# Graph attention with the context made by rows: the softmax sums as one more column of the context product, projection and transposes of x one quad later

## Chip, core and metric

One core of a Trainium2 chip. The metric is device time in microseconds; a kernel's time is the median of several executions. Engines: TensorE (PE; its weight loads are shown apart as PEld), VectorE (DVE), ScalarE (ACT), GpSimd (POOL) and SyncE (SP), which issues most transfers. Each takes its own instructions in order and waits on semaphores.

## What is computed

x is 128 graphs of 128 nodes with 128 features, fp32; adj is a 0/1 matrix for each graph. Four layers follow each other, each as x = x + layer(layernorm(x)):

```
attention 1:  q,k,v = x W.T + b (4 heads of 32);  s = q k.T * 32**-0.5;  s = -1e9 where adj == 0
              c = softmax(s) v;  o = c Wo.T + bo;  layernorm(o) * gamma + beta
experts:      8 experts, best 2 of a router
attention 2:  q,k,v = x W (8 heads of 16); same masked softmax;  c Wo + bo
recurrent:    30 steps of tanh, silu, layernorm, a 128x128 product
```

The change touches the two attentions only.

## The kernel before

x stays in SBUF as x_sb. `graph_attention` is called twice, with heads=4 (PARTS = 1, normed) and heads=8 (PARTS = 2). It works on quads of 4 graphs, 32 quads; in the second attention a quad has two parts of 4 heads each. n numbers the sets of scores: n = k in the first attention, n = 2k and 2k + 1 in the second. Every engine runs a hand-written `body(k, par)` for each quad; `quads` unrolls the first and last quads and loops over the middle ones. The order inside a body is the order of that engine's queue, and the bodies overlap by semaphores alone.

PSUM has eight banks here: four hold the scores p_s (one for each of 4 heads, 4 graphs side by side), and p_w, p_z, p_x, p_y serve everything else in turn. What is in a bank must be read before the next product into it starts, and this sets much of the order.

The way of a quad: VectorE makes statistics of x (`stats_x`, L277 to L281) two quads ahead, GpSimd the power -1/2 of the variance (L214) and the mask from adj (L215). VectorE normalises x (`normalise_x`, four operations, L288), TensorE transposes it (L447), ScalarE copies it (L610), and q, k and v are made (L432, L436, L441; copies L581 or L584, L590 or L592 and L593, L599 or L603). `scores` lays the mask (L413) and q k.T (L419; 32-row tiles) into p_s. VectorE takes the row maxima (L295, one for each bank) and splits them into a high and a low bf16 part (L304, L309); TensorE transposes both parts in two halves into p_z and p_w (L453), VectorE copies them (L316), TensorE adds them negated to the scores (`shift_scores`, L460), and ScalarE takes the exponential (L575). TensorE transposes the probabilities bank by bank (L426) and ScalarE copies them into prob_t (L570).

From prob_t two products are made one set later. `sum_prob` (L466): a matrix of ones as stationary operand for each bank, so that p_y holds every sum 32 times over, in the layout of the context's transpose (rows are features, columns are nodes). `context_product` (L473): 32 columns of v as stationary operand, a column tile of the array for each bank, prob_t moving, into p_x, already transposed. VectorE inverts p_y (512 elements in each partition, L332) and multiplies (L338) into context_t; TensorE projects (L481) into p_y; VectorE adds the bias (L347, first attention) or adds to x (L344, second). The first attention goes on with statistics (L352, L356), power on GpSimd (L227), norm (L363) and GpSimd's three operations: times gamma, plus beta, plus x (L220, L222, L224). The second has one GpSimd addition (L231).

Body of VectorE before: statistics of x, maxima, inverse sums, norm of the projection of quad k-2, scaled context, norm of x for k+2, projection of k-1 taken and its statistics; in the second attention then the maxima of the other part and the norm of x. Body of TensorE: scores, last two transposes of the old probabilities between q and k, maxima, sums, shift, context, shift, v, x's transposes, projection of k-1, first two transposes of the new probabilities.

Of the kernel before, what the change touches and what calls it, by code (L numbers as in the profile page):

```python
# [17 lines left out]
ALU = mybir.AluOpType  # L18
ACT = mybir.ActivationFunctionType
AX = mybir.AxisListType  # L20
P = 128
# [4 lines left out]
def graph_attention(nc, env, tag, x_sb, adj, weights, heads, transposed, normed, masked_op, N_GRAPHS=128, x_in=None):  # L26
# [4 lines left out]

    D = P // heads
    PARTS = heads // 4
# [9 lines left out]
    with ExitStack() as ctx:  # L43
# [17 lines left out]
        ones = sb("ones", [P, PARTS, 32])  # L61
# [9 lines left out]
        v_sb = sb("v_sb", [P, 2, PARTS, QG, P])  # L71
# [5 lines left out]
        rden = sb("rden", [P, QUAD])  # L77
# [45 lines left out]
        s_den = sem("sums_ready")  # L123
        s_pv = sem("context_product")
        s_rden = sem("rden_ready")
        s_ctx = sem("context_t_ready")
# [20 lines left out]
        def quads(eng, body):  # L147

            for j in (-1, 0, 1):
                body(2 * j, 0)  # L150
                body(2 * j + 1, 1)
            with eng.Fori(2, QUADS // 2 - 1) as j:
                body(2 * j, 0)
                body(2 * j + 1, 1)
            for j in (QUADS // 2 - 1, QUADS // 2):
                body(2 * j, 0)
                body(2 * j + 1, 1)
# [8 lines left out]
        by_head = lambda v: v.rearrange("p (a h d) -> p a h d", h=2, d=D)  # L166
# [3 lines left out]
        with nc.Block() as block:  # L170
# [26 lines left out]
            def _(pool):  # L197
                nc.gpsimd.memset(split[:], 0.0).then_inc(s_fill, 1)
                if PARTS == 2:
                    nc.gpsimd.memset(ones[:], 0.0).then_inc(s_fill, 1)  # L200
                    nc.gpsimd.memset(v_sb[:], 0.0).then_inc(s_fill, 1)
                    pool.wait_ge(s_fill, 3)
                    for part in range(2):
                        nc.gpsimd.memset(ones[:, part, part * D:(part + 1) * D], 1.0).then_inc(s_fill, 1)
                else:
                    nc.gpsimd.memset(ones[:], 1.0).then_inc(s_fill, 1)
                pool.wait_ge(s_prep, n_prep)

                def body(k, par):
                    if live(k + 2):  # L210
# [6 lines left out]
                    if normed and live(k - 2):  # L217
                        x_quad = x_sb[:, bass.ds((k - 2) * QG, QG), :]
                        pool.wait_ge(s_fn, k - 1)
                        nc.gpsimd.tensor_tensor(proj_n[:], proj_n[:], quad_row(gamma), ALU.mult).then_inc(s_fp, 1)  # L220
                        pool.wait_ge(s_fp, 2 * (k - 2) + 1)
                        nc.gpsimd.tensor_tensor(proj_n[:], proj_n[:], quad_row(beta), ALU.add).then_inc(s_fp, 1)  # L222
                        pool.wait_ge(s_fp, 2 * (k - 2) + 2)
                        nc.gpsimd.tensor_tensor(x_quad, x_quad, proj_n[:], ALU.add).then_inc(s_done, 1)  # L224
                    if normed and live(k - 1):
                        pool.wait_ge(s_fvar, k)
                        nc.gpsimd.tensor_tensor(rstd_o[:], var_o[:], minus_half[:, 0:QG], ALU.pow).then_inc(s_frstd, 1)  # L227
                    if not normed and live(k - 1):
                        x_quad = x_sb[:, bass.ds((k - 1) * QG, QG), :]
                        pool.wait_ge(s_fin, k)  # L230
# [6 lines left out]
            def _(dve):  # L237
# [30 lines left out]
                dve.wait_ge(s_fill, 5 if PARTS == 2 else 2)  # L268
# [43 lines left out]
                def take_maxima(n, half):  # L312
# [3 lines left out]
                    nc.vector.tensor_copy(max_t[rows, :], (p_w if half else p_z)[rows, 0:P]).then_inc(s_mtc, 1)  # L316
# [17 lines left out]
                def normalise_context(k):  # L334
                    dve.wait_ge(s_pv, PARTS * (k + 1))
                    dve.wait_ge(s_rden, k + 1)
                    wait(dve, s_o, k)
                    nc.vector.tensor_tensor(context_t[:], p_x[:], rden[:], ALU.mult).then_inc(s_ctx, 1)  # L338

                def take_projection(k):  # L340
                    dve.wait_ge(s_o, k + 1)
                    if not normed:
                        x_quad = x_sb[:, bass.ds(k * QG, QG), :]
                        nc.vector.tensor_tensor(x_quad, x_quad, by_graph(p_y), ALU.add).then_inc(s_fin, 1)  # L344
                        return
                    wait(dve, s_fn, k)
                    nc.vector.tensor_tensor(proj[:], by_graph(p_y), quad_row(out_bias), ALU.add).then_inc(s_fin, 1)  # L347
# [19 lines left out]
                def body(k, par):  # L367
                    if live(k + 2):
                        stats_x(k + 2)
                    if live(k):  # L370
                        maxima(PARTS * k)
                    if live(k - 1):
                        invert_sums(k - 1)
                    if normed and live(k - 2):
                        normalise_projection(k - 2)
                    if live(k - 1):
                        normalise_context(k - 1)
                    if normed and live(k + 2):
                        normalise_x(k + 2)
                    if live(k - 1):  # L380
                        take_projection(k - 1)
                    if normed and live(k - 1):
                        stats_projection(k - 1)
                    if PARTS == 2 and live(k):
                        maxima(PARTS * k + 1)
                    if not normed and live(k + 2):
                        normalise_x(k + 2)

# [1156 lines left out]
```

## Time and profile before

| | |
|---|---|
| median of 3 runs | 3371.14 us (3370.3 to 3374.31) |
| profiled execution | 3371.62 us, its span 3369.7 us |
| busy PE, DVE, ACT, POOL | 2915.1, 2727.3, 2109.1, 1731.5 us |
| mean granted clock of TensorE | 0.917 |
| chain that ended last | DVE 30%, issue 9%, all in the recurrent layer's lines |

Busy time is an average over four stages with different limits, so the page's slices come first. Each digit is the busy share of a fortieth of the span, 84 us, in tenths; PEclk is the granted clock in tenths:

```profile
PE   5666666669999978888888856999999999999999
DVE  4777777668888866666666657999999999999999
PEclk8777777789999989999999977999999999999999
```

Slices 1 to 8 are the first attention, 9 to 14 the experts, 15 to 23 the second attention, the rest the recurrent layer. The page's chain of work covers the recurrent layer and says nothing of the attentions: there the timeline of one quad has to be read.

### The profile page before, as it was taken

The page shows a single profiled execution, that of the slowest core. Times are in us where ns is not written, and L with a number is a line of the kernel's source. Part 1 is how long each engine was busy: PE and PEld are TensorE (multiplying, and loading weights), DVE is VectorE, ACT ScalarE, POOL GpSimd, SP SyncE. Part 2 cuts the span into 40 slices and gives each one's busy share as a digit, 9 for nine tenths or more (in the row PEclk, how much of TensorE's full clock was granted, in tenths as well). Part 3 has the DMA queues.
Part 4 walks back from the last instruction along what each step waited for, and adds up shares of the span by engine and source line. Part 5 has one row for each costly group of instructions (what it writes and reads, how often), then busy time and mean ns, then how long its engine had stood idle before and what let it go on. Part 6 is the DMA issues. An engine that isn't in the chain of part 4 may idle for free. (4 is left out here: it accounts for less than half of the span.)

```text
span 3369.7 us, 70085 instructions
## 1 busy us (share of the span) xinstructions
PE 2915.1 (87%) x20479; PEld 1907.5 (57%) x20479; DVE 2727.3 (81%) x7398; ACT 2109.1 (63%) x3936; POOL 1731.5 (51%) x1148
## 2 busy tenths in 40 slices
PE   5666666669999978888888856999999999999999
PEld 3444444458888855555555535555555555555556
DVE  4777777668888866666666657999999999999999
ACT  2333333324444444445454537999999999999995
POOL 2333333333333321212111125999999998888883
PEclk8777777789999989999999977999999999999999
DMA  4000000000000000000000002555555555555555
GB/s 127 13 12 12 12 13 15 0 14 0 0 0 0 0 24 11 13 9 12 9 12 9 6 3 76 195 195 195 197 198 201 201 201 198 196 197 195 197 197 176
DMA packets 132579, 281.68 MB, mean 84 GB/s; under 512 B 11760, under 2 KB 69152, under 8 KB 132512
## 3 DMA queue, kind: packets, MB, share of 16 engines
q1 hardware_dynamic: 115616, 272.44, 23.5%
q10 hardware_dynamic: 16896, 8.39, 0.9%
q8 instruction: 37, 0.61, 0.1%
q14 instruction: 30, 0.25, 0.0%
HBM read 270.49 MB, written 10.29 MB: 83 GB/s over the span
## 5 line engine op out<-in xcount | busy, mean ns | idle before, releaser
L1168 POOL TENSOR_TENSOR d_g<-d_g,d_rb 128x1024 f32<-128x1024 f32 x464 | 1083.9, 2372 | 127.9 <-DMA d_rb<-d_rstd_rows 112.7
L1369 PE MATMUL d_p_y<-d_g,d_w_main 128*128 128x512 f32 x1856 | 952.6, 595 | 0.0
L1383 PEld LDWEIGHTS d_p_gt<-ident,d_g 128*128 128x128 f32 x3840 | 450.4, 142 | 541.8 <-ACT d_g L1428 380.4
L1247 DVE BATCH_NORM_STATS2 d_stats<-d_p_gt 128x6 f32<-128x256 f32 x1920 | 713.0, 407 | 23.3 <-PE d_p_gt L1383 23.2
L1428 ACT ACTIVATE d_g<-d_th,d_bias 128x512 f32<-128x512 f32 x928 | 667.0, 719 | 12.1 <-DVE d_th L1240 0.9
L1240 DVE SCALAR_TENSOR_TENSOR d_th<-d_th,d_p_y 128x512 f32<-128x512 f32 x960 | 634.7, 661 | 4.1 <-ACT d_th L1424 4.1
L1424 ACT ACTIVATE d_th<-d_p_y,d_bias 128x512 f32<-128x512 f32 x928 | 625.6, 674 | 0.3 <-PE d_p_y L1369 0.3
L1383 PE MATMUL d_p_gt<-ident,d_g 128*128 128x128 f32 x3840 | 592.6, 278 | 0.1
L295 DVE TENSOR_REDUCE a_row_max<-a_p_s 128x4 f32<-128x512 f32 x384 | 253.6, 682 | 231.6 <-PE a_p_s L419 231.6
L570 ACT COPY a_prob_t<-a_p_w 128x512 f32<-128x512 f32 x288 | 169.5, 588 | 406.0 <-PE a_p_w L426 405.9
L214 POOL TENSOR_TENSOR a_rstd<-a_var,minus_half 128x4 f32<-128x4 f32 x64 | 65.3, 1020 | 670.9 <-PE a_p_s L419 630.0
L897 DVE SCALAR_TENSOR_TENSOR x_sb<-m_p_y,m_combine,x_sb 128x128 f32 (+1 forms) x1024 | 310.9, 342 | 68.8 <-PE m_p_y L939 56.0
L986 ACT ACTIVATE m_hidden<-m_p_h,m_cols 128x512 f32<-128x512 f32 x256 | 176.5, 689 | 225.9 <-PE m_p_h L931 225.9
L575 ACT ACTIVATE a_prob<-a_p_s 128x512 f32<-128x512 f32 x384 | 208.3, 594 | 134.9 <-PE a_p_s L460 134.9
L1369 PEld LDWEIGHTS d_p_y<-d_g,d_w_main 128*128 128x128 f32 x1856 | 280.1, 191 | 6.3 <-issue 4.7
L939 PEld LDWEIGHTS m_p_y<-m_w_sb,m_hidden 128*128 128x128 f32 x2048 | 266.4, 191 | 25.6 <-issue 3.6
L939 PE MATMUL m_p_y<-m_w_sb,m_hidden 128*128 128x128 f32 x2048 | 271.0, 275 | 0.0
L447 PE MATMUL a_p_w<-ident,a_xn 128*128 128x128 f32 x256 | 57.0, 362 | 210.2 <-DVE a_xn L288 210.2
L332 DVE RECIPROCAL a_rden<-a_p_y 128x512 f32<-128x512 f32 x64 | 214.9, 3358 | 12.0 <-PE a_p_y L466 10.0
L426 PE MATMUL a_p_w<-ident,a_prob 128*128 128x128 f32 x1152 | 209.1, 311 | 4.8 <-ACT a_prob_t L570 3.3
L481 PE MATMUL a_p_y<-a_w_o,a_context_t 128*128 128x128 f32 x512 | 104.8, 371 | 101.3 <-DVE a_context_t L338 101.3
L426 PEld LDWEIGHTS a_p_w<-ident,a_prob 128*128 128x128 f32 x1152 | 145.3, 157 | 64.7 <-ACT a_prob_t L570 44.0
(192 smaller groups left out, 4216.6 us busy)
## 6 DMA issues: line engine op xcount, KB each, us to landing
d_rb<-d_rstd_rows SPq DMA_DIRECT2D x464, 512.0 KB, 5.5
a_adj_in<-in_adj_dram SPq DMA_DIRECT2D x64, 256.0 KB, 2.8
out_dram<-d_out_sb ACTq DMA_DIRECT2D x32, 256.0 KB, 2.4
d_rstd_rows<-d_rstd_row SPq DMA_DIRECT2D x116, 16.0 KB, 1.4
m_w_sb<-in_L_ffn_w_dram SPq DMA_DIRECT2D x2, 512.0 KB
x_sb<-in_x_dram SPq DMA_DIRECT2D x1, 256.0 KB, 2.8
a_w_raw<-in_L_gnn_Wq_dram SPq DMA_DIRECT2D x2, 64.0 KB, 2.1
a_w_raw<-in_L_gnn_Wk_dram SPq DMA_DIRECT2D x2, 64.0 KB, 2.1
```

Source lines behind the costliest of these rows:

```text
L295: ins = nc.vector.tensor_reduce(out=row_max[:, t], in_=p_s[:, t], axis=AX.X, op=ALU.max)
L332: nc.vector.reciprocal(rden[:], p_y[:]).then_inc(s_rden, 1)
L426: last = nc.tensor.transpose(bank[:, graph(g)], prob[:, t, g, :], ident[:])
L897: last = nc.vector.scalar_tensor_tensor(out=x_tile, in0=p_y[:, e % 2, t, :], scalar=combine[:, par, t, e:e + 1], in1=x_tile, op0=ALU.mult, ...
L939: last = nc.tensor.matmul(p_y[:, e % 2, t, :], hidden[:, e % 2, t * P:(t + 1) * P], w2_sb[:, e, :], start=True, stop=True)
L1168: nc.gpsimd.tensor_tensor(g[:, c, :], g[:, c, :], rb[:, buf, :], ALU.mult).then_inc(s_gs, 1)
L1240: nc.vector.scalar_tensor_tensor(out=th[:, b, cols(u)], in0=th[:, b, cols(u)], scalar=0.01, in1=p_y[:, b, cols(u)], op0=ALU.mult, op1=ALU. ...
L1247: ins = nc.vector.bn_stats(stats[:, q % 2, (j * CT + t) // 2].rearrange("p a s -> p (a s)"), p_gt[:, t * P:(t + 2) * P].rearrange("p (a c) ...
L1369: nc.tensor.matmul(p_y[:, c % 2, cols(u)], w_main[:], g[:, c, cols(u)], start=True, stop=True).then_inc(s_y, 1)
L1383: ins = nc.tensor.transpose(p_gt[:, t * P:(t + 1) * P], g[:, c, t * P:(t + 1) * P], ident[:])
L1424: nc.scalar.activation(th[:, b, cols(u)], p_y[:, b, cols(u)], ACT.Tanh, bias=col).then_inc(s_th, 1)
L1428: nc.scalar.activation(g[:, c, cols(u)], th[:, c % 2, cols(u)], ACT.Silu, bias=col).then_inc(s_g, 1)
```

## The change

- The context is made by rows: 128 columns of probabilities (transposed, one graph, one head) are the stationary operand, and the moving one is v of that head with a column of ones behind it (v_ones, 33 or 17 columns). The result has nodes as rows, and the last column of each head is the sum. `sum_prob` and the matrices of ones go. The products go in two halves to p_w and p_z (first attention) or into p_w by part (second).
- VectorE inverts the sums (8 or 16 elements a partition) and scales, in two shares, into `context`; four transposes and a ScalarE copy make context_t (`transpose_context`, `take_context`).
- The projection is made at quad k-2 and taken at k-3 (first) or k-2 (second); the norm of the projection, its statistics and GpSimd's operations follow at k-3 and k-4, GpSimd's three now ahead of the power and mask in its body. Statistics of x are made three quads ahead in the first attention and the norm of x stands behind the maxima.
- The transposed maxima of both halves, x's transposes and q (in the second attention v) use p_y, k and v (second: k), the transposed context and the projection p_x. The bodies are written out apart for the two attentions.

Cut to its core:

```diff
-        v_sb = sb("v_sb", [P, 2, PARTS, QG, P])
+        v_ones = sb("v_ones", [P, 2, QG, heads, VW])
-        rden = sb("rden", [P, QUAD])
+        rden = sb("rden", [P, 2, 8 * PARTS])
+        context = sb("context", [P, 2, QG, P])
...
-                def invert_sums(k):
-                    dve.wait_ge(s_den, PARTS * (k + 1))
-                    nc.vector.reciprocal(rden[:], p_y[:]).then_inc(s_rden, 1)
...
+                    dve.wait_ge(s_pv, 2 * k + share + 1)
+                    nc.vector.reciprocal(inverse, src[:, :, :, D]).then_inc(s_rden, 1)
+                    dve.wait_ge(s_rden, 2 * k + share + 1)
+                    wait(dve, s_ct, k - 1)
+                    each = rden[:, share].rearrange("p (g h a) -> p g h a", h=4, a=1)
+                    nc.vector.tensor_tensor(dst, src[:, :, :, 0:D], each.broadcast_to([P, 2 * PARTS, 4, D]),
+                                            ALU.mult).then_inc(s_norm, 1)
...
-                        last = nc.tensor.matmul(p_y[tile(t), :], ones[:, part, :], prob_t[:, t],
-                                                start=part == 0, stop=part == PARTS - 1)
...
+                        for t in range(4):
+                            last = nc.tensor.matmul(dst[:, i, t], prob_t[:, t, g, :], v_ones[:, par, g, PARTS * t + part],
+                                                    start=True, stop=True)
...
+                def transpose_context(k, par):
+                    pe.wait_ge(s_norm, 2 * (k + 1))
+                    for g in range(QG):
+                        last = nc.tensor.transpose(p_x[:, graph(g)], context[:, par, g, :], ident[:])
+                    last.then_inc(s_ct, 1)
```

VectorE's bodies after:

```
first:   take_projection(k-3), maxima(k), normalise_x(k+2), normalise_context(k-1, 0), (k-1, 1),
         stats_projection(k-3), stats_x(k+3), normalise_projection(k-3)
second:  maxima(2k), normalise_x(k+1), normalise_context(k-1, 1), stats_x(k+2), take_projection(k-2),
         maxima(2k+1), normalise_context(k, 0)
```

TensorE's bodies after:

```
first:   scores, context transposed (k-2), probabilities 2 (k-1), q (k+1), probabilities 3, k (k+1), maxima 0,
         context graphs 0 and 1 (k-1), shift 0, maxima 1, context graphs 2 and 3, shift 1, v (k+1), x (k+2),
         probabilities 0 and 1 (k), project (k-2)
second:  scores, context transposed (k-2), probabilities 2, v (k), probabilities 3, maxima 0, context, shift 0,
         maxima 1, context, shift 1, project (k-2), x (k+1), probabilities 0 and 1;
         scores, probabilities 2, q (k+1), probabilities 3, k (k+1), maxima 0, context, shift 0, maxima 1, context,
         shift 1, wait for the scaled context, probabilities 0 and 1
```

## Rows read from the trace of the kernel before

**Rows 1.** One tile (inverse sums), both attentions: ns min/median/max, first and last start us.
```profile
L332 DVE RECIPROCAL a_rden<-a_p_y x32: 3356/3358/3358, 57.9 to 677.3; 128x512 f32<-128x512 f32 x32
...
L332 DVE RECIPROCAL a_rden<-a_p_y x32: 3356/3358/3358, 1246.7 to 1978.9; 128x512 f32<-128x512 f32 x32
```
**Rows 2.** Timeline, first attention, one quad: start, length us, engine, idle before.
```profile
300.50 3.36 DVE L332 RECIPROCAL a_rden<-a_p_y 128x512 f32<-128x512 f32 x1
...
303.77 1.02 DVE L363 TENSOR_SCALAR a_proj_n<-a_proj,a_stats_o,a_rstd_o 128x128 f32<-128x128 f32 x4
...
304.88 1.26 POOL L220 TENSOR_TENSOR a_proj_n<-a_proj_n,a_gamma 128x512 f32<-128x512 f32 x1 [5.92 <-DVE a_proj_n L363]
305.31 3.71 DVE L288 TENSOR_SCALAR a_xn<-x_sb,a_stats,a_rstd 128x128 f32 x4
...
307.68 1.26 POOL L224 TENSOR_TENSOR x_sb<-x_sb,a_proj_n 128x512 f32 x1 [0.20 <-POOL a_proj_n L222]
...
309.07 1.11 PE L447 MATMUL a_p_w<-ident,a_xn 128*128 128x128 f32 x4 [6.52 <-DVE a_xn L288]
...
316.21 1.29 DVE L295 TENSOR_REDUCE a_row_max<-a_p_s 128x4 f32<-128x512 f32 x2 [1.11 <-PE a_p_s L419]
...
318.86 0.24 PE L453 MATMUL a_p_z<-ident_bf,a_split 128*64 128x128 bf16 x1
...
320.96 3.36 DVE L332 RECIPROCAL a_rden<-a_p_y 128x512 f32<-128x512 f32 x1
```
**Rows 3.** Stretches: us, busy PE, PEld, DVE, ACT, POOL (count), PEclk, DMA, GB/s.
```profile
300.50:321.00 20.50, 13.98 (x133) 9.46 (x128) 14.83 (x28) 6.99 (x14) 7.76 (x6) 0.75 0.04 13
302.90:309.10 6.20, 0.03 (x1) 0.03 (x1) 6.12 (x10) 0.28 (x1) 3.78 (x3) 0.62 0.00 0
309.10:314.60 5.50, 5.50 (x23) 4.69 (x24) 2.09 (x6) 1.76 (x3) 0.90 (x1) 0.50 0.00 0
...
1579.00:1602.90 23.90, 20.16 (x232) 12.54 (x225) 15.08 (x32) 11.70 (x24) 4.23 (x3) 0.93 0.04 11
...
1608.30:1611.70 3.40, 3.40 (x13) 1.95 (x11) 0.69 (x1) 1.17 (x2) 0.00 (x0) 0.50 0.00 0
```
**Rows 4.** Timeline of TensorE, second attention, one quad.
```profile
1589.37 1.02 PE L432 MATMUL a_p_y<-a_xn_t,a_w_q 128*128 128x512 f32 x2
...
1590.23 0.63 PE L426 MATMUL a_p_w<-ident,a_prob 128*128 128x128 f32 x4
...
1596.05 1.03 PE L413 MATMUL a_p_s<-a_mask,ident_bf 128*128 128x512 bf16 x4
...
1597.00 1.17 PE L419 MATMUL a_p_s<-a_k_t,a_q_t 32*128 32x128 f32 x32
...
1601.96 0.39 PE L460 MATMUL a_p_s<-a_selector,a_max_t 32*128 32x512 bf16 x2
...
1602.45 1.08 PE L473 MATMUL a_p_x<-a_prob_t,a_v_sb 128*32 128x128 f32 x32
...
1607.27 1.13 PE L481 MATMUL a_p_y<-a_w_o,a_context_t 128*128 128x128 f32 x8 [2.83 <-DVE a_context_t L338]
```
**Rows 5.** Timeline of TensorE, mixture of experts: the router's product.
```profile
762.00 0.96 PE L963 MATMUL m_p_lg<-m_cols,m_xn_t 128*128 128x8 f32 x8
...
762.84 0.48 PE L929 MATMUL m_p_h<-m_xt_hi,m_w_lo 128*128 128x512 f32 x1
```
**Rows 6.** Timeline of VectorE, second attention.
```profile
1592.19 0.17 DVE L304 TENSOR_SCALAR a_split<-a_row_max 128x8 bf16<-128x8 f32 x1
...
1592.48 1.08 DVE L309 SCALAR_TENSOR_TENSOR a_split<-a_row_max,a_split 128x8 bf16<-128x8 f32 x1
...
1594.22 1.12 DVE L288 TENSOR_SCALAR a_xn<-x_sb,a_stats,a_rstd 128x128 f32 x4
...
1595.49 0.76 DVE L277 BATCH_NORM_STATS2 a_stats<-x_sb 128x6 f32 x2 [0.15 <-DVE a_xn L288]
```
**Rows 7.** Timeline of ScalarE, second attention: the copy of v.
```profile
1599.77 0.65 ACT L603 COPY a_v_sb<-a_p_z 128x256 f32<-128x256 f32 x2 [0.38 <-PE a_p_z L441]
```

More of the change, by code:

```diff
@@ L151, in quads @@
                 body(2 * j + 1, 1)
-            with eng.Fori(2, QUADS // 2 - 1) as j:
+            with eng.Fori(2, QUADS // 2 - 2) as j:
                 body(2 * j, 0)
                 body(2 * j + 1, 1)
-            for j in (QUADS // 2 - 1, QUADS // 2):
+            for j in range(QUADS // 2 - 2, QUADS // 2 + 2):
                 body(2 * j, 0)
@@ L198, in _ @@
                 nc.gpsimd.memset(split[:], 0.0).then_inc(s_fill, 1)
[L199 to L206, printed above, removed]
+                nc.gpsimd.memset(v_ones[:], 1.0).then_inc(s_fill, 1)
                 pool.wait_ge(s_prep, n_prep)
                 def body(k, par):
+                    if normed and live(k - 4):
+                        x_quad = x_sb[:, bass.ds((k - 4) * QG, QG), :]
+                        pool.wait_ge(s_fn, k - 3)
+                        nc.gpsimd.tensor_tensor(proj_n[:], proj_n[:], quad_row(gamma), ALU.mult).then_inc(s_fp, 1)
+                        pool.wait_ge(s_fp, 2 * (k - 4) + 1)
+                        nc.gpsimd.tensor_tensor(proj_n[:], proj_n[:], quad_row(beta), ALU.add).then_inc(s_fp, 1)
+                        pool.wait_ge(s_fp, 2 * (k - 4) + 2)
+                        nc.gpsimd.tensor_tensor(x_quad, x_quad, proj_n[:], ALU.add).then_inc(s_done, 1)
                     if live(k + 2):
@@ L593, in take_k, with take_v @@
                         nc.scalar.activation(k_t[:, 1], p_x[:], ACT.Copy, scale=part_of[:, 1:2]).then_inc(s_k, 1)
[L595 removed]
+                def take_v(k, par, bank):
                     act.wait_ge(s_vmm, k + 1)
[L597 to L604 removed]
+                    wait(act, s_pv, 2 * (k - 1))
+                    nc.scalar.copy(v_ones[:, par, :, :, 0:D],
+                                   bank[:].rearrange("p (g h c) -> p g h c", g=QG, h=heads)).then_inc(s_v, 1)
                 def take_xn(k):
@@ new lines, in take_xn, with take_context, first_body @@
+                    nc.scalar.copy(xn_t[:], p_y[:]).then_inc(s_xtc, 1)
+                def take_context(k):
+                    act.wait_ge(s_ct, k + 1)
+                    wait(act, s_o, k)
+                    nc.scalar.copy(context_t[:], p_x[:]).then_inc(s_ctc, 1)
+                def first_body(k, par):
+                    if live(k - 1):
+                        take_prob(k - 1, 0)
+                        take_prob(k - 1, 1)
+                    if live(k - 2):
+                        take_context(k - 2)
+                    if live(k - 1):
+                        take_prob(k - 1, 2)
+                    if live(k + 1):
+                        take_q(k + 1)
+                    if live(k - 1):
+                        take_prob(k - 1, 3)
+                    if live(k + 1):
+                        take_k(k + 1)
+                    if live(k):
+                        for t in range(4):
+                            exponentials(k, t)
+                    if live(k + 1):
+                        take_v(k + 1, 1 - par, p_x)
+                    if live(k + 2):
+                        take_xn(k + 2)
```

410 lines of the change are left out of this document (235 added, 175 removed).

## The prediction

> **What bounds the kernel now.** I read the page's 40 slices first: the two attention stages (about 31 to 692 us and 1213 to 1995 us) are where TensorE is least busy. The change touches only them, so the 500 us of the mixture of experts and the 1330 us of the recurrent stage stay as they are. The view of one tile, the inverse sums, gives one reciprocal per quad of graphs, so its first and last start measure a quad: 31 steps from 57.9 to 677.3 us are 19.98 us each in the first attention, 31 steps from 1246.7 to 1978.9 us are 23.62 us each in the second [rows 1].
>
> Then I followed one quad in the timeline. In the first attention it is a loop that hands over between VectorE and TensorE, with nothing beside it [rows 2]. From the reciprocal at 300.50 VectorE never rests until 309.0: reciprocal 3.36, norm of the old projection (1.02), context scaled, and x normalised, which takes 3.71 us. Only then can TensorE transpose x (309.07, after 6.52 us idle), and behind it in its queue stand projection, two transposes of the probabilities, masks and scores. Those end at 316.2, where VectorE starts the row maxima; these end in the next reciprocal at 320.96. The sum is the period, 20.46 us.
>
> Three things in this loop are dearer than they need be. The reciprocal runs over 512 elements a row. The four normalisations of x take 3.71 us since three GpSimd operations of 1.26 us run in the same time (304.88 to 308.94 [rows 2]); in the second attention, where none does, the same four take 1.12 us [rows 6]. And TensorE, after its rest, works from 309.1 to 314.6 at a granted clock of 0.50, so 1.2 instead of 2.4 GHz [rows 3].
> By the Trainium skill (GPSIMD Engine Reference, Specifications) GpSimd shares its SBUF interfaces with VectorE and contends with VectorE instructions in a 2-port mode or with two SBUF inputs; the trace agrees (3.71 against 1.12 us), also for an 8-element operation with two such inputs, which took 1.08 us beside a GpSimd operation [rows 6].
>
> The second attention has two sets of scores per quad and is nearer to TensorE's own work: 20.16 us busy of 23.90 [rows 3]. Its one large hole is 2.83 us before the projection, which waits for reciprocal and scaled context [rows 4], and 3.4 us at half clock after it [rows 3].
>
> **The change, part by part.** (1) Removed: the context product in 32-column tiles (32 matmuls, 1.08 us with their tail [rows 4]), the sums by a matrix of ones (8 matmuls, which I take as long), and the reciprocal over 512 elements. Per quad TensorE loses 2.0 us in the first attention and 4.0 in the second, VectorE 3.36 in each.
>
> (2) Added: the context product with 128 columns of probabilities as weights and 33 (or 17) moving columns. In fp32 every product is two instructions, so 32 weight loads and matmuls per set of scores. No such row exists in attention; the nearest on both sides are the router's product with 8 moving columns, 8 pairs from 762.00 to 762.84 [rows 5], so 0.105 us a pair at full clock, and the transposes with 128 columns, 4 from 1590.23 within 0.63 us with their tail [rows 4], 0.11 a pair. The ends agree: the weight load sets the pace. 16 pairs are 1.7 us, and 0.25 before the next, differently tiled product can start: 1.95 us for each half, 3.9 per set, against 2.0 for what it replaces.
> The Trainium skill (TensorEngine Tiling, When to Use Tiling) advises the reverse of this step: with 32 moving columns swap the operands and use column tiling four times. By its factor of four the product would go from 1.0 to 4.0 us, which the pace of rows 5 bears out; it speaks against this half of the change in the stage that TensorE bounds.
>
> (3) Added: 4 transposes of the context (0.48), a ScalarE copy (about 0.6, as v's in [rows 7]), and on VectorE per share a reciprocal of 8 or 16 elements and a scaling of 256. The trace has no reciprocal of this size; the bounds are 0.17, an 8-element operation [rows 6], and 3.36. With 3.36/512 = 6.6 ns an element added to 0.17 I take 0.2 and 0.25, nearer to the row of that size. The scaling of 256 elements is 0.42, half of a 512-element pass (two in 1.29 [rows 2]) and its start. VectorE in the first attention: 14.83 us a quad [rows 3], less 3.36, less 2.6 (x beside no GpSimd work), plus 0.9, gives 9.8.
>
> (4) Moved: x's normalisation, its transposes and the projection. First attention, TensorE's queue at full clock [rows 4]: masks 0.95 (1596.05 to 1597.00), scores 1.1, six groups of 4 transposes 2.9, q and k 0.86 each, shift and transposed maxima twice 0.49 (1601.96 to 1602.45), context 3.9, v and projection 0.9 and 0.96 (8 pairs each): 13.4 us. I walked the waits along it: from the end of the scores to the first transposed maxima TensorE now has 3.2 us of work, VectorE needs 2.65 + 0.15 for the split maxima (316.21 to 318.86 [rows 2]), so this wait closes; v, projection and the last transposes (2.8 us) cover the scaled contexts; the probabilities' copies on ScalarE (about 8 us a quad) keep pace.
> What is late next is GpSimd. Its gamma, beta and x operations now wait for the projection's norm at the end of VectorE's body and run for 4.05 us into the next maxima. There the split of the maxima (a few elements, with SBUF inputs) is held as in rows 6. The loop: from the first to the second transposed maxima 2.4 (context half, shift), their copy and x 1.8, two scaled contexts 1.4, statistics of the projection 1.0 (0.76 [rows 6] and the variance), GpSimd's power 1.1, norm 1.1, GpSimd's three 4.1, then the held split, a row maximum and the low part 1.0: 13.9, which I round to 13.95 for hand-overs. I take **13.95 us**, bounds 13.4 (no contention) and 14.95 (the power of GpSimd that follows holds it for 1.0 more).
>
> Second attention, same durations. First half: 2.05 for masks and scores; from there to the context product 3.4, since v's copy (0.65 [rows 7]) and the last probabilities' copy behind it on ScalarE are late by 0.7; context, shifts, maxima 4.7; projection, transposes of x and of two tiles 2.4: 12.6. Second half: 2.05, then 2.95, then 4.4 up to the last context product's issue; its result must be inverted and scaled before the bank is free (0.25 + 0.42 + hand-overs), 0.55 us in which TensorE stands, then 1.0: 11.2. Total **23.8 us**, equal to the 23.85 of a steady quad before: the 2.83 us hole and the half clock go, and 3.9 us of added weight loads, 0.5 of transposes and the new waits take their place.
>
> (5) The end: the last quads now drain one body later, and GpSimd does three quads' work of 4 us with a power between. From the last probabilities to the end of the first attention I count 25 us against about 18 (the last reciprocal starts at 677.3). Plus 7 us, once. In the second the added and removed pieces cancel. Filling v_ones hides behind the weights' transfers.
>
> **The sum**, against the profiled execution's 3371.6 us (3371.14 is the median): first attention 31 x 19.98 = 619.4 before; 31 x 13.95 = 432.5 after, less 4 for the last quads, which lack projections of a next one: 191 saved, less 7 is 184. Second: 0. 3371.6 - 184 = **3188 us** (13.4 us and no stalls in the second: 3188 - 17 - 30 = 3141).
>
> **Rivals.** *A, the forecast*, chance 0.55.
> *B, the clock falls at the new product.* In the trace the clock fell while TensorE rested and stayed at half through 5.5 us of full work before it rose (302.9 to 309.1, then to 314.6 [rows 3]). No stretch there is filled with matmuls of 33 columns behind 128-column loads, where the array streams for a quarter of the time; the chip may take that for rest. In the second attention one low stretch lasts 3.4 us [rows 3], costing half of it, 1.7. Three such groups per pair of quads make 93; if two thirds of them trigger one: 93 x 0.67 x 1.7 = 105 us, 3293. Chance 0.26.
> By the Trainium skill (TensorE: Matmul & The Clock Gate, Part 1) a monitor sets the clock by how busy the array has been; whether a weight load counts, no row here shows.
> *C, the in-order queues lose more than I found*: one further microsecond in each quad of both stages, for instance the held split in the first and the scaled context in the second: 62 us, 3250. Chance 0.11.
> *D, slower*: the clock is low throughout each group, so a group costs 3.9 more: first attention 17.9, second 31: 3371.6 - 65 + 7 + 229 = 3543. It decides from 184/93 = 2.0 us a group, so if more than about half of each runs at 1.2 GHz. Against it: the low level in rows 3 follows rest, not work. Chance 0.06.
> *E, the change doesn't do what it says*: a reciprocal costs 3.36 us whatever its size; no other size stands in the trace. Then VectorE alone needs 9.8 + 6.3 = 16.1 us in the first attention, 16.4 with waits, and the second takes 3.1 more: 31 x (3.6 - 3.1) is gained, 7 lost, about 3363. Against it: VectorE's other operations shrink with their size (0.17 for 8 elements [rows 6], 0.65 for 512 [rows 2]). Chance 0.02.
>
> **How the numbers follow.** The likeliest is A, 3188, whose own range is 3141 to 3235. To hold 8 in 10 the range must reach B's centre: 3141 to 3300; beyond lie D, E and the upper part of B. A difference within 0.2% (7 us) can't be told from none. Faster: A, B, C and part of E, 0.92; same 0.02; slower 0.06.
>
> **What would show it.** A quad of 14 us in the first attention, the granted clock at 1.00 throughout, the four normalisations of x in 1.1 us, VectorE waiting before the maxima rather than TensorE before x. The 32 pairs of a context product in 3.5 to 3.9 us; twice that, or a granted clock of 0.50 behind them, speaks for B or D. In the second attention a period near 23.8 with a wait of about half a microsecond before the transposes that follow the last context product. The forecast fails first if the clock does not hold or if the queue's waits in the second attention are longer than my 1.3 us.

## The result and the profile after

The kernel with the change takes 3431.7 us (median; 3429.55 to 3438.22) beside 3372.72 us of the kernel before: a ratio of 1.018 (95% interval 1.016 to 1.020). It is 59 us slower where 184 us less were forecast.

The stages tell that two things happened at once:

| stage | before | after | change |
|---|---|---|---|
| first attention | 689.9 us | 566.0 us | -123.9 |
| experts | 510.6 | 510.8 | +0.2 |
| second attention | 784.4 | 970.5 | +186.1 |
| recurrent | 1382.3 | 1380.1 | -2.2 |

A steady quad, by the starts of the row maxima of quads 5 to 25, went from 20.48 to 15.88 us in the first attention and from 23.77 to 29.23 us in the second. The page's slices of after show where (same columns as those of before ahead of the prediction):

```profile
PE   6999996999998999999999985999999999999999
DVE  4666664888886434444444437999999999999999
PEclk8888886999998778777777766999999999999999
```

Slices 1 to 7 are the first attention, 8 to 12 the experts, 13 to 24 the second. TensorE is now busy throughout both attentions, VectorE 60% of the first and 40% of the second: the loop of [rows 2] is gone. But PEclk, 9 in most slices of the second attention before, is 7 in most of them. The view of stretches says the same with numbers (us; busy of PE, PEld, DVE, ACT, POOL with counts; granted clock; DMA share; GB/s), here the middle of each attention, of after:

```profile
50.00:530.00 480.00, 479.14 (x3571) 389.78 (x3569) 288.01 (x851) 222.11 (x391) 220.88 (x170) 0.82 0.05 15
1110.00:2040.00 930.00, 898.35 (x6526) 714.80 (x6524) 376.64 (x993) 386.40 (x691) 126.42 (x90) 0.76 0.03 8
```

and the same of before:

```profile
50.00:650.00 600.00, 413.79 (x3638) 278.25 (x3637) 431.78 (x787) 206.20 (x357) 221.46 (x171) 0.75 0.04 12
1240.00:1960.00 720.00, 606.49 (x6700) 383.95 (x6697) 452.25 (x903) 353.08 (x671) 123.85 (x88) 0.93 0.03 10
```

After the change TensorE rests for 0.9 us of 480 and 32 us of 930, and its mean granted clock is 0.82 and 0.76. The granted clock has only two levels here, 1.00 and 0.50; in these stretches it is at the half level for 36% and 47% of the time (before: 49% and 13%). In the first attention the low clock of before lay behind a rest, as in [rows 3]; now it lies between instructions that follow each other without a gap.

Where it falls shows in the timeline of a quad. First attention, after (start, length, engine, operation; in brackets idle time before it and what ended it):

```profile
309.28 1.97 PE L484 MATMUL a_p_w<-a_v_ones,a_prob_t 128*128 128x33 f32 x16
...
311.68 1.97 PE L484 MATMUL a_p_z<-a_v_ones,a_prob_t 128*128 128x33 f32 x16
...
312.11 1.11 DVE L284 TENSOR_SCALAR a_xn<-x_sb,a_stats,a_rstd 128x128 f32 x4
313.26 0.21 DVE L336 RECIPROCAL a_rden<-a_p_w 128x8 f32<-128x8 f32 x1
313.50 0.42 DVE L340 TENSOR_TENSOR a_context<-a_p_w,a_rden 128x256 f32<-128x256 f32 x1
...
313.90 2.06 PE L455 MATMUL a_p_x<-a_w_v,a_xn_t 128*128 128x128 f32 x8
...
315.75 1.06 PE L461 MATMUL a_p_y<-ident,a_xn 128*128 128x128 f32 x4
```

and the granted clock of the stretches from the scores on, in the same columns as above, with the low stretch of the quad before ahead of them:

```profile
298.20:303.80 5.60, 5.60 (x28) 5.60 (x28) 2.78 (x10) 3.19 (x6) 3.44 (x3) 0.51 0.00 0
...
304.82:309.28 4.46, 4.46 (x51) 2.99 (x50) 3.15 (x7) 2.30 (x5) 3.55 (x3) 1.00 0.00 0
309.28:313.90 4.62, 4.62 (x39) 4.02 (x38) 2.48 (x11) 1.71 (x3) 0.00 (x0) 1.00 0.19 57
313.90:317.20 3.30, 3.30 (x17) 3.30 (x16) 3.01 (x12) 2.02 (x4) 1.04 (x1) 0.51 0.00 0
317.24:320.40 3.16, 3.16 (x42) 2.49 (x45) 1.10 (x3) 1.26 (x3) 2.54 (x2) 0.98 0.00 0
```

In this quad the two context halves themselves run at full clock, each in 1.97 us with its tail (1.95 were forecast). Behind them TensorE runs at 0.51, the 1.2 GHz level, with no idle time in between: v takes 2.06 us (a projection of 8 pairs, each a weight load and its matmul, took 1.13 in [rows 4]) and four transposes 1.06 (0.63 there). In the second attention the clock can fall within the product. TensorE of after:

```profile
1564.71 1.96 PE L484 MATMUL a_p_w<-a_v_ones,a_prob_t 128*128 128x17 f32 x16 [0.17 <-ACT a_prob_t L651]
...
1567.38 3.60 PE L484 MATMUL a_p_w<-a_v_ones,a_prob_t 128*128 128x17 f32 x16
...
1571.44 2.08 PE L498 MATMUL a_p_x<-a_w_o,a_context_t 128*128 128x128 f32 x8
```

The same 16 pairs take 1.96 us at full clock and 3.60 us at half.

How long the clock stays low varies from quad to quad. Between 50 and 530 us there are 30 low stretches, one in each quad: 20 of 6.8 us and 10 of 3.4. Quads with a short one, like the one shown, take 14.8 us from row maxima to row maxima, the others 16.4. On VectorE everything is as cheap as forecast: x's four normalisations 1.11 us beside 3.71 in [rows 2], the small reciprocals 0.21 us at their longest in this quad beside 3.36 in [rows 1].

### The profile page after: what moved, and what is told of

Read it like the earlier page. It is cut to its first block and busy times, and to the rows that moved or that the text cites. A ratio compares the mean times of both kernels' runs of the same rounds, so it can differ in the third digit from the quotient of the medians.

```text
span 3429.9 us, 69233 instructions
## 1 busy us (share of the span) xinstructions
PE 3255.9 (95%) x19967; PEld 2345.0 (68%) x19967; DVE 2485.2 (72%) x7526; ACT 2144.2 (63%) x3968; POOL 1732.3 (51%) x1145
## 5 line engine op out<-in xcount | busy, mean ns | idle before, releaser
L484 PE MATMUL a_p_w<-a_v_ones,a_prob_t 128*128 128x17 f32 (+1 forms) x2560 | 374.9, 293 | 7.0 <-ACT a_prob_t L651 7.0
L484 PEld LDWEIGHTS a_p_w<-a_v_ones,a_prob_t 128*128 128x128 f32 x2560 | 358.4, 224 | 21.2 <-ACT a_prob_t L651 11.9
L651 ACT COPY a_prob_t<-a_p_w 128x512 f32<-128x512 f32 x192 | 112.9, 588 | 108.4 <-PE a_p_w L442 107.5
L312 DVE CAST a_max_t<-a_p_y 64x128 bf16<-64x128 f32 x192 | 56.2, 293 | 158.4 <-PE a_p_y L467 158.4
L442 PE MATMUL a_p_w<-ident,a_prob 128*128 128x128 f32 x768 | 156.2, 340 | 13.6 <-DVE a_context L340 13.6
L691 ACT COPY a_context_t<-a_p_x 128x512 f32<-128x512 f32 x64 | 37.5, 586 | 203.3 <-PE a_p_x L492 203.3
```

The lines of the kernel that those rows point to most:

```text
L484: last = nc.tensor.matmul(dst[:, i, t], prob_t[:, t, g, :], v_ones[:, par, g, PARTS * t + part], start=True, stop=True)
```

## Experiments

**1. More moving columns, and nothing else.** If the array's short streaming behind long weight loads lowers the clock, wider moving operands should raise it again, at no cost as long as the weight load sets the pace. v_ones gets a tail, and each product moves 128 (or 64) columns from its head on; what it writes too far right is overwritten by the next product.

```diff
-        v_ones = sb("v_ones", [P, 2, QG, heads, VW])
+        v_ones = sb("v_ones", [P, 2, QG * heads * VW + COLS - VW])
...
-                            last = nc.tensor.matmul(dst[:, i, t], prob_t[:, t, g, :], v_ones[:, par, g, PARTS * t + part],
+                            last = nc.tensor.matmul(bank[:, at:at + COLS], prob_t[:, t, g, :], v_ones[:, par, of:of + COLS],
```

COLS = 128:

> The changed kernel, but each product of the context takes 128 moving columns instead of 33 or 17: the v and ones of the head and whatever stands behind them. The columns beyond the head's own are overwritten by the next product into the bank, or never read, so what is computed stays the same, and so do the counts of instructions, weight loads and waits. In the changed kernel's trace the clock was at half in 36% of the first attention and 48% of the second, and it fell in the second half of nearly every context product, although TensorE was issuing without a rest. Theory 1 (the clock falls because the array has few moving columns behind each weight load): a 128-column pair has the same pace as a short one, 0.11 us, so the products take the same 1.9 us at full clock, and the clock stays at 1.00: 15.7 us a quad becomes about 14.0 in the first attention and 29.3 becomes 23.8 in the second, together 3432 - 54 - 170 = 3208 us (3190 to 3235). Theory 2 (the clock falls for another reason: waits at the ends of the products, or the many weight loads themselves): within 10 us of 3432. Theory 3 (the order and the waits of the queues cost the time, and the clock is a by-product): at most 30 us better than 3432.

Measured: 3172.37 us (3170.93 to 3173.37), 0.941 of the kernel before (0.939 to 0.942). That is Theory 1, and 18 us better than the low end of its range. First attention 493.3 us, second 782.4; quads 13.55 and 23.65 us, where 14.0 and 23.8 were expected. In the middle stretches below the clock is at half for 2 us of 410 and for none of 680; what is left of the low clock lies at the stages' ends. The stretches in the middle of each attention, padded kernel:

```profile
50.00:460.00 410.00, 406.36 (x3574) 315.99 (x3573) 305.26 (x851) 214.96 (x391) 220.36 (x170) 1.00 0.06 18
1060.00:1740.00 680.00, 648.91 (x5974) 508.19 (x5974) 349.41 (x922) 346.72 (x634) 119.49 (x85) 1.00 0.04 11
```

and its rows for the product and what follows it:

```profile
300.73 2.05 PE L486 MATMUL a_p_z<-a_v_ones,a_prob_t 128*128 128x128 f32 x16
...
302.71 0.39 PE L476 MATMUL a_p_s<-a_selector,a_max_t 32*128 32x512 bf16 x2
...
303.03 1.16 PE L457 MATMUL a_p_x<-a_w_v,a_xn_t 128*128 128x128 f32 x8
```

Four or seven times as many columns move, and the shift behind the product starts 1.98 us after its first pair instead of 1.90 (309.28 to 311.18 in the kernel after). Dearer by 0.13 us a set (1.95 and 1.98 us for the two halves, 1.90 each before), the padded kernel is 259 us faster than the change as it was made. The counts and the order of the instructions are the same and only the width differs, so what the narrow products cost comes through the clock. TensorE now rests for 3.6 us of 410 in the first attention: that stage is bound by TensorE's own queue. From v to the masks, the stretch that ran at half clock, the padded kernel takes 3.20 us (303.03 to 306.23); the kernel after took 4.85 in the quad shown (313.90 to 318.75) and 6.01 in the one before it (297.85 to 303.86). The padded kernel beats both the kernel before and the change as made, and none of the runs that follow gave a faster one that computes everything.

COLS = 64:

> The same with 64 moving columns. Theory 1: somewhere from e1 (if 64 is enough to hold the clock) to halfway back: 3208 to 3320 us, and the share of time at half clock tells which. Theory 2 and 3: as the changed kernel, 3432 within 10.

Measured: 3219.62 us (3215.11 to 3221.48), 0.955 (0.953 to 0.957), inside Theory 1's range; first attention 491.5 us, second 826.6. In their middle stretches (50 to 460 and 1060 to 1780 us) the clock is at half for 0.2% and 12% of the time:

```profile
1060.00:1780.00 720.00, 688.93 (x6030) 545.34 (x6029) 351.82 (x925) 350.09 (x638) 120.91 (x86) 0.94 0.04 10
```

With 64 columns the clock holds in the first attention and not always in the second, where two sets of products stand in a quad. In the stand-alone stretch of experiment 3, it held throughout with 64 columns; what decides in the second attention isn't settled.

**2. The stages apart.** The first attention as changed, the second as before; once with the narrow product, once padded to 128.

```diff
-    graph_attention(nc, env, "a1_", ...)
+    graph_attention_2(nc, env, "a1_", ...)
```

> The change in the first attention alone; the second is the one of the kernel before. From the two traces the first attention went from 689.9 to 566.0 us (124 less) and the second from 784.4 to 970.5 (186 more). If the stages are independent, as their barriers suggest: 3372 - 124 = 3248 us (3242 to 3254). A rival in which the first attention's gain hangs on something shared (code loading, the state of the clock at a stage's start) would give over 3260.

Measured: 3250.94 us (3249.49 to 3252.36), 0.964 (0.962 to 0.966): stages of 567.0 and 786.8 us, inside the expected 3242 to 3254.

> The first attention changed and with 128 moving columns as in e1, the second as before. Theory 1: e3 less 54 us, 3194 (3180 to 3210), with a quad of 14.0 us in the first attention, which is also what the forecast's loop over GpSimd's three operations gives. Theory 2 and 3: as e3, 3248. If the quad comes out at 13.4 instead of 14.0, GpSimd's hold on VectorE is not in the loop.

Measured: 3178.43 us (3177.18 to 3178.77), 0.942 (0.941 to 0.944): stages of 492.1 and 788.7 us, just below Theory 1's 3180 to 3210. The quad of 13.55 us fell between the two values that were to decide about GpSimd's hold; experiment 4 decides it. The stages are independent within 5 us. Narrow, the second attention of the change costs 181 us (3431.7 - 3250.9); padded, it is worth 6 us (3178.4 - 3172.4). So what the prediction gave the second attention, 23.8 us a quad and neither gain nor loss, holds once the clock does (23.65).

**3. The clock by itself.** The kernel before with a stretch of TensorE alone between second attention and recurrent layer: fp32 products of a 128-column stationary and a moving operand of c columns, back to back with no wait in them, 120 products (240 pairs) of a width with 80 products of 128 columns ahead of each.

```diff
+            for count, widths in segments:
+                for n in range(count):
+                    c = widths[n % len(widths)]
+                    last = nc.tensor.matmul(p_c[:, 0:c], x_sb[:, n % 8, :], x_sb[:, 8 + n % 8, 0:c], start=True, stop=True)
```

> The kernel before, with a stretch of TensorE work of its own between the second attention and the recurrent layer; it only times itself, its results are not used. Stretches of 120 fp32 products (240 weight loads of 128 columns and matmuls) with 17, 33, 48, 64 and 96 moving columns, each behind 80 products of 128 columns; at the end 160 products that alternate 4 of 17 with 4 of 128, and 160 that alternate 16 with 16. No semaphore, no other engine and no rest is in it. Theory 1 (moving columns behind a weight load decide the clock): every pair takes 0.11 us at full clock whatever its width; the granted clock falls to 0.50 within the stretches of 17 and 33 and stays at 1.00 at 96 and 128; 64, which held in the first attention of e2 and partly fell in the second, lies at the edge; alternating 4 with 4 holds, 16 with 16 falls. Theory 2 (waits or rests in the attention's queue): 1.00 in all of them, since nothing waits. The stretch takes about 340 us if the clock holds, more where it falls.

Measured: one run, 3793.99 us, 420 more than the kernel before beside it, where the stretch was expected to take about 340 if the clock held. The stretches, in the columns as above: 17, 33, 48, 64 and 96 columns, then 4 products of 17 and 4 of 128 in turn, then 16 and 16 in turn:

```profile
2003.80:2051.10 47.30, 47.30 (x243) 47.30 (x241) 0.00 (x0) 0.00 (x0) 0.00 (x0) 0.54 0.00 1
2071.25:2117.80 46.55, 46.55 (x243) 46.55 (x241) 0.00 (x0) 0.00 (x0) 0.00 (x0) 0.55 0.00 1
2137.10:2184.50 47.40, 47.40 (x243) 47.40 (x241) 0.00 (x0) 0.00 (x0) 0.00 (x0) 0.54 0.00 1
2204.50:2231.25 26.75, 26.75 (x243) 26.75 (x241) 0.00 (x0) 0.00 (x0) 0.00 (x0) 1.00 0.00 1
2249.20:2275.90 26.70, 26.70 (x242) 26.70 (x241) 0.00 (x0) 0.00 (x0) 0.00 (x0) 1.00 0.00 1
2293.80:2329.60 35.80, 35.80 (x323) 35.80 (x323) 0.00 (x0) 0.00 (x0) 0.00 (x0) 1.00 0.00 1
2347.40:2391.30 43.90, 43.90 (x322) 43.90 (x322) 0.00 (x0) 0.00 (x0) 0.00 (x0) 0.81 0.00 1
```

TensorE and its weight loads are busy for all of each stretch, so nothing rests. 240 pairs with 64 or 96 columns take 26.7 us, 0.111 us a pair, at 1.00; with 17, 33 or 48 columns they take 46.6 to 47.4 us, at 0.54 or 0.55. So Theory 2 is refuted, and Theory 1 came as expected at 17, 33, 96 and in both mixtures. The number of moving columns is all that tells the first five stretches apart. As a pair takes the same 0.111 us with 64 as with 96, these runs don't separate the number of columns from the share of the time in which they stream. It isn't each product for itself: with four narrow ones between four wide ones the clock held, with 16 between 16 it was at half for 17.1 of 43.9 us. In the kernel after, the narrow ones come 8 products (16 pairs) at a time with shift and maxima between, and there it fell too.

**4. GpSimd's hold on the split of the maxima.** GpSimd's work can hold an operation of VectorE's, which then doesn't end before GpSimd's does ([rows 6]). In the forecast the first attention ends in a loop through GpSimd (13.95 us a quad), not in TensorE's own 13.4. Padded kernel with GpSimd's addition of beta left out of the first attention (the output lacks beta):

```diff
-                        nc.gpsimd.tensor_tensor(proj_n[:], proj_n[:], quad_row(beta), ALU.add).then_inc(s_fp, 1)
```

> e1 with GpSimd's addition of beta left out in the first attention (so beta is missing from the result): two operations of 1.27 us instead of three run into VectorE's maxima. If GpSimd's hold on VectorE (the 1.03 us split of 8 elements in e1's quad, and TensorE's 0.2 us wait behind it) is in the loop, as forecast, the quad of the first attention goes from 13.55 to 13.4: 32 x 0.15 = 5 us, and 1.3 once at the end, so e1 less 6 (3164 to 3168). If not: within 2 us of e1.

Measured: 3166.11 us (3165.24 to 3166.84), 0.939 (0.937 to 0.940), a quad of 13.39 us. That is 0.16 us a quad less than padded, about 5 of the 6 us, as expected. The hold is in the loop, but TensorE's queue, 13.4 us by the forecast, is nearly as long as that loop. In the padded kernel it is seen here:

```profile
309.59 1.27 POOL L215 TENSOR_TENSOR x_sb<-x_sb,a_proj_n 128x512 f32 x1 [0.20 <-POOL a_proj_n L213]
...
309.87 1.03 DVE L302 TENSOR_SCALAR a_split<-a_row_max 128x8 bf16<-128x8 f32 x1 [0.15 <-DVE a_row_max L293]
...
311.61 0.11 PEld L469 LDWEIGHTS a_p_y<-ident_bf,a_split 128*64 128x64 bf16 x1 [0.90 <-DVE a_split L307]
```

An 8-element operation takes 1.03 us beside a GpSimd operation and ends with it, at 310.9 (0.17 without, [rows 6]), and the maxima's weights wait 0.90 us; most of that stands in front of work that TensorE still had in its matmul queue (L452, 310.52 for 1.02 us).

The padded kernel with GpSimd's three operations behind power and mask instead of ahead of them:

```diff
-                    if normed and live(k - 4):
-                        x_quad = x_sb[:, bass.ds((k - 4) * QG, QG), :]
...
+                    if normed and live(k - 4):
+                        x_quad = x_sb[:, bass.ds((k - 4) * QG, QG), :]
```

> e1 with GpSimd's three operations on the projection put back behind the power and the mask in its body, as in the kernel before. They then run from about 3.1 us behind the scores' end to 7.1 and meet the norm of x at 5.9, which they hold for a microsecond or more, but the split of the maxima is free. My loop says that the norm of x has that microsecond to spare before TensorE's transposes of x, so the quad becomes 13.4: 3 to 6 us less than e1. The rival, that a held norm of x is what made the kernel before slow and does so again: the quad grows by a microsecond, 30 us more than e1.

Measured: 3175.54 us (3174.16 to 3176.92), 0.941 (0.940 to 0.942), a quad of 13.60 us. Neither the expected gain nor the rival's loss came. The hold moved with them. VectorE of this kernel:

```profile
301.82 2.12 DVE L286 TENSOR_SCALAR a_xn<-x_sb,a_stats,a_rstd 128x128 f32 x4
...
312.32 1.28 DVE L302 TENSOR_SCALAR a_split<-a_row_max 128x8 bf16<-128x8 f32 x1
```

x's normalisation now takes 2.12 us in place of 1.11, and a split is still held (1.28): in both places that were tried, the 4 us of GpSimd work lie beside something of VectorE's.

**5. What the dear reciprocal alone was worth.** The kernel before, with its order and its tiled context product; the reciprocal covers 16 of the 512 elements, and the other inverses are one, so the context is not normalised there.

```diff
-                    nc.vector.reciprocal(rden[:], p_y[:]).then_inc(s_rden, 1)
+                    nc.vector.reciprocal(rden[:, 0:16], p_y[:, 0:16]).then_inc(s_rden, 1)
```

> The kernel before, with the inverse of the sums taken over 16 of its 512 elements (the other inverses stay at one, so the context is not normalised): nothing else changes, TensorE's queue least of all. It measures how much of the change's gain is the dear reciprocal on the loop, apart from the new order. If the reading of the two timelines of before is right, 3.1 us leave the loop of the first attention (20.5 to 17.4 a quad, or down to 15.5 where TensorE's shorter rest keeps its clock up) and TensorE's 2.8 us hole before the projection in the second closes, with the half clock behind it (23.8 to 19.4): 3372 less 99 less 140 = 3133 us, from 3065 to 3185. If something else in the queue is late at once (the rival by which the change's gain came from its new order): 3300 or more.

Measured: 3116.03 us (3113.68 to 3116.62), 0.924 (0.922 to 0.925), inside the expected 3065 to 3185: stages of 563.0 and 653.7 us, quads of 16.66 and 19.65. The reciprocal took 3.10 us less (3.36 to 0.26), the quads 3.8 and 4.1 us less. The middle of the second attention of this kernel:

```profile
1120.00:1710.00 590.00, 559.22 (x6607) 350.29 (x6608) 354.24 (x891) 346.52 (x662) 123.93 (x88) 1.00 0.04 12
```

The hole in front of the projection [rows 4] and the half clock behind it [rows 3] went together: 1.00, where it was 0.93. That fits the quads' losing more than the reciprocal did; in the first attention, too, the mean clock rose, from 0.75 to 0.86. Set beside this kernel, the padded change shows what its two halves are worth: in the first attention it is 3.1 us a quad better than this kernel (13.55 against 16.66); in the second it is 4.0 us worse (23.65 against 19.65). The prediction counted 3.9 us of added weight loads and 0.5 of transposes there, which fits; but the two kernels also differ in their order, so the split isn't shown. In the second attention, then, the change spends on TensorE all that the cheap reciprocal gains.

**6. The inverse on ScalarE.** So I tried to have that cheap inverse with the tiled product: first attention padded, second as before, with 1/sum made on ScalarE as a logarithm and an exponential of its negative, between the second and third exponential of a set.

```diff
-                    nc.vector.reciprocal(rden[:], p_y[:]).then_inc(s_rden, 1)
+                    nc.scalar.activation(lnden[:], p_y[:], ACT.Ln).then_inc(s_lnd, 1)
...
+                    nc.scalar.activation(rden[:], lnden[:], ACT.Exp, scale=-1.0).then_inc(s_rden, 1)
```

> A version out of what the runs showed: the first attention as in e1, the second as in the kernel before, with its inverse of the sums made on ScalarE (logarithm from PSUM, exponential of its negative: two operations of about 0.6 us between the second and the third exponential) instead of VectorE's reciprocal of 3.36 us. e8 gave 19.65 us a quad in the second attention with a short reciprocal. ScalarE is busy 12 of 23.8 us there, so the two operations find room; the scaled context comes about 1 us later than in e8: 19.7 to 20.7 us a quad. 3172 - 782 + 660 = 3050 us (3040 to 3090). If logarithm and exponential need a table load at each change (1.28 us by the load seen once in the experts' stage, two for each quad): up to 3125. If the place in ScalarE's queue holds up the next exponentials: 3100.

Measured: 3227.22 us (3222.59 to 3228.61), 0.957 (0.955 to 0.959); the second attention is 840.4 us long, 52 us more than with the reciprocal (experiment 2), and its middle is at half clock for 20% of the time (14% there). A miss: 3050 us were expected, and 3125 with table loads. Part of the reason stands in ScalarE's timeline:

```profile
1279.44 1.28 ACT L614 ACT_TABLE_LOAD   x1
1280.73 0.60 ACT L614 ACTIVATE a_lnden<-a_p_y 128x512 f32<-128x512 f32 x1
1281.35 1.28 ACT L617 ACT_TABLE_LOAD   x1
1282.64 0.63 ACT L617 ACTIVATE a_rden<-a_lnden 128x512 f32<-128x512 f32 x1
```

The two functions cost the 1.2 us that were counted, and each brings a table load of 1.28 us, 52 of them in 26 quads. For 3.8 us a quad ScalarE takes nothing else, and the last two banks of probabilities wait in its queue. The quad is 5.9 us longer than in experiment 5 (25.59 against 19.65); the loads take 2.6 us of ScalarE's time a quad, and how the 5.9 divide between them, the waits in the queue and the lower clock wasn't tested. The Trainium skill (ScalarE: Activation LUTs, Table sets: the hidden batching unit) says that exponential and logarithm share one set and need one load; this trace shows one at each change between them. Other places for the pair weren't tried.

## Why the prediction was wrong

It failed in one step: the sum of part (4) takes every duration at full clock, and no term stands for what the new product does to the clock. The runs show that term as 259 us, more than the 200 that the rest of the change saves (3372.7 - 3172.4). In order of its parts:

**What bounds the kernel** was read rightly. With the loop gone and the clock held, the first attention fell from 20.48 to 13.55 us a quad. The 500 and 1330 us given to the other two stages are 510.6 and 1382.3 in the table above; neither enters the sum.

**Part (2), the price of a pair**, was right at full clock and left out what the pairs do to the clock. 1.95 us a half were forecast; 1.97 are measured with its tail, and 1.90 up to the next product. The router's product [rows 5], from which the price came, is 8 pairs with 8 columns; no row had a long run of narrow products, and the text said so under B. All durations of part (4) were taken at full clock, and of all assumptions in the sum this one weighed most.

**Part (3)** held: reciprocals 0.2 and 0.25 forecast, 0.21 and 0.26 measured, scaling 0.42 and 0.42. The view of the inverse's tile, of after (ns min/median/max, first and last start):

```profile
L336 DVE RECIPROCAL a_rden<-a_p_w x96: 207/257/258, 59.0 to 2040.7; 128x16 f32<-128x16 f32 x64, 128x8 f32<-128x8 f32 x32
L340 DVE TENSOR_TENSOR a_context<-a_p_w,a_rden x96: 423/425/426, 59.3 to 2041.0; 128x256 f32<-128x256 f32 x96
```

**Part (4)** held once the clock did: 13.95 forecast and 13.55 measured, 23.8 and 23.65. (The terms written down for the second attention's second half add up to 10.95 us, not 11.2, so its quad would be 23.5; that is as near.) Within the first, the loop through GpSimd was given 0.55 us above TensorE's own 13.4; experiment 4 shows 0.16. The wait before the transposes behind the last context product was forecast at about half a microsecond and is 0.56 and 0.57 us in the padded kernel's timeline (0.35 and 0.56 in that of after).

**Part (5)**, plus 7 and less 4 us at the ends: the first attention of the padded kernel is 196.6 us shorter than before. 184 were forecast. By first and last start, as in [rows 1], a quad fell from 19.98 to 13.39 us (31 steps from 60.1 to 475.2), 204 us in all, so the ends lost 8, where 3 (7 less 4) were counted. The 13.95 was set against a mean over all steps (19.98), so its counterpart is 13.39: the quad was 0.56 us too long, 17 us in all, of which the ends took back 5.

**The sum** of forecast A comes near the padded kernel: 3188 us against 3172. For the change as made it misses 244 us: 259 for the clock, less 15.

**Rival B** is what happened, with the right mechanism and two wrong sizes. It had a low stretch of 3.4 us behind two of three groups, each costing half of it, 1.7 us: 105 us in all, and a chance of 0.26. Measured are 259 us over 93 groups, 2.8 each: by stages (566.0 - 493.3) / 31 = 2.3 us in the first attention, (970.5 - 782.4) / 62 = 3.0 in the second. The first wrong size is how many groups bring the clock down: not two of three but practically each (30 low stretches in the 30 quads of the first stretch shown above, one a group in the second too). The other is how long it stays down. The 3.4 us came from a stretch at half clock that follows a rest [rows 3]; here it is 5.7 us a group on average in the first attention (36% of 15.88) and 6.9 in the second (47% of 29.23, over two groups), and half of that, 2.8 and 3.4 us, is what it can cost at most.

**Rival D**, slower, named the point at which the sign turns, 2.0 us a group, and rightly: the measured 2.8 lies above it, between B's 1.7 and D's own 3.9. What I held against it, that the low level in [rows 3] follows rest and not work, was true of the rows and no argument: none of them had this kind of work. D at 0.06 and a range that ended at B's centre were therefore too low: the range left out what B costs once its size is off by a factor of two.

The Trainium skill (TensorE: Matmul & The Clock Gate, Why this matters for your kernels) advises, for matmuls with few rows (small M), another loop or padding M, since the clock otherwise falls and rises with each tile. What is padded here is another size, the moving columns, and TensorE hardly waits (0.9 us of 480), so the runs neither test that advice nor its reason.

**Rival C** (longer queues' waits) did not come: the padded quads are shorter than forecast (13.55 and 23.65 us). **Rival E**, a reciprocal that costs 3.36 us whatever its size, is refuted by the 0.21 us.

**The advice on tiling** that the prediction weighed (the Trainium skill, TensorEngine Tiling, When to Use Tiling: swap the operands and tile) agrees with experiment 5: in the second attention the tiled product takes 19.65 us a quad once the reciprocal is cut short, and the product by rows 23.65. That kernel doesn't normalise its context, and experiment 6 found no way to do so at that price.

## What to carry over

A price per instruction that is read at full clock is only half of a price: of a new kind of TensorE work ask also what it leaves the array doing, and where long weight loads come with few moving columns, look at the granted clock behind them before anything else. Where the weight load sets the pace, padding the moving operand with columns that are overwritten costs next to nothing, and here it turned a ratio of 1.018 into 0.941. Where the bounds of a mechanism lie on both sides of the sign, a range must reach to its far end, not to the centre of its mild case.

## What the runs showed of the hardware

- TensorE without any rest was at 1.2 GHz for 43.2 of 47.3, 41.6 of 46.6 and 43.4 of 47.4 us in the stretches whose products move 17, 33 and 48 columns, and at 2.4 GHz throughout in those with 64 and 96 (experiment 3). In [rows 3] the half clock had followed a rest.
- At full clock a pair of an fp32 weight load of 128 columns and its matmul takes 0.111 us whether it moves 64 or 96 columns (experiment 3). At half clock 16 narrow pairs took 3.60 us, 0.22 a pair (the kernel after, 1567.38).
- Most of VectorE's time for a reciprocal goes by its size: 0.21 us for 8 elements a partition, 0.26 for 16, 3.36 for 512, about 6.25 ns an element (the kernel after, and [rows 1]).
- An exponential behind a logarithm and the reverse cost a table load of 1.28 us each time (experiment 6).
- GpSimd's 512-element tensor_tensor operation (1.27 us) held VectorE's 8-element one until it ended, also when that has one SBUF input (L302, 1.03 and 1.28 us in experiment 4), not only with two as in [rows 6].
